# A graph layer on one core: softmax of the last pass made chunk by chunk, one deeper gather ring, and three stages joined

## The reference

```python
xn = layernorm(x)
x = x + relational_gat(xn, src, dst, edge_type)     # 8 heads, softmax over the edges of a node, floored at 0
      + linear_attention(xn)
x = x + shared_mlp(layernorm(x)) + routed_experts(layernorm(x))   # 1024 hidden, 2 of 8 experts
xn = layernorm(x)
h = relu(gcn_conv(xn, src, dst) )                   # self loops, degree norm
x = x + relu(gat_conv(h, src, dst)) + (y := xn + channel_attention(xn)) + mlp(layernorm(y))   # 1 head; 768 hidden
x = x + capacity_ffn(x)                             # top half of the tokens by a router
```

## Time and profile before

| | |
|---|---|
| median of 3 runs | 3726.47 us (3723.8 to 3730.51) |
| the profiled execution | 3732.52 us, span 3730.7 us |
| granted clock, mean | 0.813 of full |
| PE busy | 2577.2 us (69%) |
| DVE busy | 1415.3 us (38%) |
| ACT busy | 1062.6 us (28%) |
| POOL busy | 1368.2 us (37%) |
| instructions | 44933 |

### The profile page before, as it was taken

The page is one execution under the profiler, slowest core; times in us unless marked ns, Lnnn a source line. Parts: engine busy times, 40 slices in busy tenths (PEclk is TensorE's granted clock), DMA queues, the critical chain, the costliest instruction groups (busy, mean ns, idle before and its releaser), DMA issues. The chain is left out here.

```text
span 3730.7 us, 44933 instructions
## 1 busy us (share of the span) xinstructions
PE 2577.2 (69%) x12282; PEld 1921.9 (52%) x12282; DVE 1415.3 (38%) x3375; ACT 1062.6 (28%) x2733; POOL 1368.2 (37%) x1383
## 2 busy tenths in 40 slices
PE   2599626666655778999974577675635667676697
PEld 2465314444434657888863344453434555555575
DVE  4655224544556200000014111222547344444767
ACT  1022213333343111322322243334301333333321
POOL 1022356665640310000013666666230666565110
PEclk7599857777886889999986788787755888888899
DMA  4045433332320102565643333333264222222101
GB/s 161 19 150 184 145 82 93 90 90 81 91 64 25 51 20 84 187 196 179 193 135 103 112 91 91 89 90 92 72 188 142 85 82 84 78 84 78 60 1 35
DMA packets 241044, 370.74 MB, mean 99 GB/s; under 512 B 65140, under 2 KB 171073, under 8 KB 240836
## 3 DMA queue, kind: packets, MB, share of 16 engines
q0 software_dynamic: 63632, 179.42, 16.5%
q1 hardware_dynamic: 147694, 157.81, 13.4%
q10 hardware_dynamic: 29510, 31.06, 2.4%
HBM read 306.56 MB, written 61.61 MB: 99 GB/s over the span
## 5 line engine op out<-in xcount | busy, mean ns | idle before, releaser
L1089 POOL DMA_INDIRECT ag_rows<-rows,e_bsrc x392 | 387.7, 989 | 399.5 <-SPq L1100 257.0
L1307 POOL DMA_INDIRECT at_rows<-values,e_brow x392 | 396.9, 1013 | 282.8 <-SPq L1318 142.1
L2458 POOL DMA_INDIRECT cm_rows<-rows,e_bsrc x392 | 371.0, 946 | 227.7 <-issue 104.9
L1383 PE MATMUL at_part<-at_msg,x 128*128 128x265 f32 x880 | 308.0, 500 | 184.9 <-DVE at_msg L1538 114.7
L1114 PE MATMUL banks<-ag_msg,ag_one 128*128 128x258 f32 x880 | 262.6, 439 | 194.4 <-DVE ag_msg L1146 139.6
L1383 PEld LDWEIGHTS at_part<-at_msg,x 128*128 128x128 f32 x880 | 200.0, 245 | 271.0 <-issue 123.9
L1114 PEld LDWEIGHTS banks<-ag_msg,ag_one 128*128 128x128 f32 x880 | 185.9, 219 | 253.3 <-DVE ag_msg L1146 123.6
L2538 PE MATMUL cm_part<-cm_rows,cm_one 128*128 x880 | 260.3, 444 | 58.3 <-issue 35.1
L1979 POOL DMA_INDIRECT je_y<-expert_out,slots x50 | 48.4, 968 | 648.0 <-POOLq L75 613.9
L2660 DVE TENSOR_TENSOR h<-h,cm_part 128x256 f32 x220 | 92.3, 420 | 461.7 <-PE cm_part L2538 210.0
L2538 PEld LDWEIGHTS cm_part<-cm_rows,cm_one 128*128 128x128 f32 x880 | 184.9, 222 | 122.3 <-issue 96.3
(11 more groups left out here) (602 smaller groups left out, 4264.3 us busy)
## 6 DMA issues: line engine op xcount, KB each, us to landing
x_w<-in_L_ffn_W1p SPq DMA_DIRECT2D x32, 1024.0 KB
x_w<-in_L_ffn_W2p SPq DMA_DIRECT2D x32, 1024.0 KB
values<-p_hv ACTq DMA_DIRECT2D x25, 1088.0 KB
p_brow<-local_row SPq DMA_DIRECT2D x44, 320.0 KB, 3.6
xn_acc<-local_row SPq DMA_DIRECT2D x44, 320.0 KB
xn_acc<-low_row SPq DMA_DIRECT2D x49, 256.0 KB
expert_in<-z_z POOLq DMA_DIRECT2D x8, 1024.0 KB
x_xr<-expert_in SPq DMA_DIRECT2D x32, 256.0 KB, 2.7
```

The lines of the kernel that those rows point to most:

```text
L1089: pool.indirect_dma_start(rows[:, b % slots, k, :], None, table, bass.IndirectOffsetOnAxis(index[:, k, b:b + 1], 0)).then_inc(gathered[b % ...
L1307: pool.indirect_dma_start(rows[:, b % RING, k, :], None, table, bass.IndirectOffsetOnAxis(e.block_row[:, k, b:b + 1], 0)).then_inc(gathere ...
L1383: last = pe.matmul(part[:, n % deep, 0:wide], one[:, n // U % 2, k, n % U, :], msg[:, n % 4, k, :], start=(k == 0), stop=(k == K2 - 1))
L2458: pool.indirect_dma_start(rows[:, b % SLOTS, k, :], None, table, bass.IndirectOffsetOnAxis(e.block_src[:, k, b:b + 1], 0)).then_inc(gather ...
```

## The change

1. `find_groups` no longer makes the tables for `segment_softmax` (DVE L604 to L615, L642 to L660) nor stores `low_row`.
2. `finish_attention0`, `layer_norm` "ln1_", the weight loads and `route_and_share` become one stage. SP starts the loads at its start. DVE `prepare(g)` divides, joins and normalises one group of five tiles at a time (POOL takes the power); PE transposes the first five tiles and starts the MLP; the other 20 tiles are turned between the MLP's steps, the logits come at step 27, the exponential at 29, and the placing matmuls after tile 10 where they came after tile 2.
3. The convolution's ring has 20 blocks, asked back nine late (14 and five before).
4. The `ff1_` weights are loaded by SP in the last pass, behind its 44 loads of rows.
5. `score2`, `segment_softmax` and `aggregate` go; `attend_last` takes their place. Only the 44 destination units are matched; the source score travels as the 257th column of `rows2` (a row is 1028 B, before 1024 B) and ACT fetches it for each pair; the softmax is made online in 14 chunks as in `attend`, with masks brought by DMA from ACT's queue; the ring is 28 blocks freed 22 late. The exponentials now stand between the Gelus of the ride, and an ACT_TABLE_LOAD comes with each switch: 54 by the written order. The ride's down product has one PSUM bank where it had two, and `gcn_to_gat` splits four operations less on `own`.

The diff, cut to its core:

```diff
-SLOTS = 14
-SLOTS2 = 20
-LAG = 5
+SLOTS = 20
+LAG = 9
@@ find_groups @@
-            sp.wait_ge(low_made, 1)
-            for h in range(2):
-                sp.dma_start(low_row[h * BH:(h + 1) * BH], low[:, h, :]).then_inc(rows_out, 16)
...
-            link(dve.tensor_scalar(edge[:], edge[:], NEG, None, ALU.mult))
-            link(dve.tensor_copy(e.step[:], edge[:]))
...
-            link(dve.tensor_scalar(e.over_this[:], this[:], -1.0, -NEG, ALU.add, ALU.mult))
             dve.wait_ge(runs_kept, 1)
@@ MlpRide.multiply @@
                 pe.wait_ge(self.shaped, (lo // 2 + 1) * self.fb)
-                if t >= 2:
-                    pe.wait_ge(self.added, t - 1)
-                else:
-                    pe.wait_ge(*self.gate)
+                if t:
+                    pe.wait_ge(self.added, t)
                 for f in range(self.fb):
-                    last = pe.matmul(self.down_ps[:, t % 2, 0:D], self.hid[:, f, (t - lo) * P:(t - lo + 1) * P], w2[:, f, :],
+                    last = pe.matmul(self.down_ps[:, 0:D], self.hid[:, f, (t - lo) * P:(t - lo + 1) * P], w2[:, f, :],
                                      start=(f == 0), stop=(f == self.fb - 1))
                 last.then_inc(self.down, 1)
+def attend_last(nc, c, e, target, local_row, table, acc, ride, loads):
+    deep = 3
+    wide = D + 2
+    step_of = {lo - LEAD + i: (pc, lo, m, i) for pc, (lo, m) in enumerate(CHUNKS) for i in range(LEAD + 1)}
...
+        @block.sync
+        def _(sp):
+            units = local_row.rearrange("(b g) e -> b (g e)", g=U)
+            for v in range(UNITS):
+                if v >= 3:
+                    sp.wait_ge(matcher, v - 2)
+                sp.dma_start(brow[:, v % 3, :], units[v:v + 1].broadcast_to([P, BT * P])).then_inc(row_in[v % 3], 16)
+            for to, of in loads:
+                sp.dma_start(to, of, allow_slow_non_contiguous=True).then_inc(ride_loaded, 16)
+            for b in range(NB):
+                sp.wait_ge(gathered[b % RING], 16 * K2 * (b // RING + 1))
+                sp.sem_inc(ready, 1)
+                if FREE <= b < NB - RING + FREE:
+                    pairs = sp.value_load(e.upto[0:1, b - FREE:b - FREE + 1], min_val=1, max_val=G)
+                    sp.wait_ge(weighted, pairs)
+                    sp.sem_inc(freed, 1)
+
+        @block.tensor
...
+            for v in range(UNITS):
+                match(v)
+            for n in range(-LEAD, G):
+                if n in step_of:
+                    softmax(*step_of[n])
+                if n < 0:
+                    continue
+                if n == 0:
+                    pe.wait_ge(ride_loaded, 16 * len(loads))
+                ride.multiply(pe, n)
+                if n % U == 0:
+                    pe.wait_ge(hot, n // U + 1)
+                pe.wait_ge(weighted, n + 1)
+                if n >= deep:
+                    pe.wait_ge(summed, n - deep + 1)
+                for k in range(K2):
+                    last = pe.matmul(part[:, n % deep, 0:wide], one[:, n // U % 2, k, n % U, :], msg[:, n % 4, k, :], start=(k == 0), stop=(k == K2 - 1))
+                last.then_inc(multiplied, 1)
+        @block.scalar
...
+            def take_mask(pc):
+                lo, m = CHUNKS[pc]
+                for h, first, past in pieces[pc]:
+                    act.dma_start(mask[first - lo:past - lo, pc % 2, :], e.pair[first - h * HALF:past - h * HALF, h, :]).then_inc(mask_in[pc % 2], 16)
+            def fetch(n):
+                pc, j = n // CH, n % CH
+                if n % U == 0:
+                    blks[:] = several(nc, mybir.EngineType.Activation, e.blk, n, U, NB - 1, waited=True)
+                b = blks[n % U]
+                if j == 0 and pc >= 2:
+                    act.wait_ge(scored, pc - 1)
+                act.wait_ge(ready, b + 1)
+                act.copy(src[:, pc % 2, :, j:j + 1], rows[:, bass.ds(b % RING, 1), :, D:D + 1].squeeze(1)).then_inc(copied, 1)
...
+                if i == 3:
+                    act.wait_ge(shifted, pc + 1)
+                    act.activation(s[0:m], s[0:m], ACT.Exp, scale=-1.0).then_inc(exped, 1)
+                if i == 4:
+                    if pc >= 2:
+                        act.wait_ge(weighted, CHUNKS[pc - 1][0])
+                    act.wait_ge(back_turned, pc + 1)
+                    act.copy(w[:, pc % 2, :, 0:m, :].rearrange("p k n z -> p z k n"),
+                             turn[:, 0:2 * K2 * m].rearrange("p (z k n) -> p z k n", z=2, k=K2)).then_inc(w_kept, 1)
+                    if pc + 2 < len(CHUNKS):
+                        take_mask(pc + 2)
+                if i == 6:
+                    act.wait_ge(faded, pc + 1)
+                    if pc:
+                        act.wait_ge(rescaled, pc)
+                    act.activation(fade[:], small[:, 0:1], ACT.Exp).then_inc(fade_kept, 1)
...
+            act.wait_ge(ride_loaded, 16 * len(loads))
+            for n in range(FREE - LEAD):
+                fetch(n)
+            for n in range(-LEAD, G):
+                if n == -LEAD + 1:
+                    hots(0)
+                if n >= 0 and n % U == 0 and n + U < G:
+                    hots(n // U + 1)
+                if n + FREE < G:
+                    fetch(n + FREE)
+                if n in step_of:
+                    softmax(*step_of[n])
+                if n >= 0:
+                    ride.shape(act, n)
         @block.vector
...
+            def weigh(n, b):
+                pc, j = n // CH, n % CH
+                if n >= 4:
+                    dve.wait_ge(multiplied, n - 3)
+                if j == 0:
+                    dve.wait_ge(w_kept, pc + 1)
+                row = rows[:, bass.ds(b % RING, 1), :, 0:D].squeeze(1)
+                of = w[:, pc % 2, :, j, :]
+                dve.tensor_copy(msg[:, n % 4, :, D:wide], of)
+                dve.tensor_tensor(msg[:, n % 4, :, 0:D], row, of[:, :, 0:1].broadcast_to([P, K2, D]), ALU.mult).then_inc(weighted, 1)
+            def add_up(n, tile):
+                if n:
+                    dve.wait_ge(summed, n)
+                if n % CH == 0:
+                    pc = n // CH
+                    dve.wait_ge(fade_kept, pc + 1)
+                    dve.tensor_scalar(acc[:, tile, :], acc[:, tile, :], fade[:, 0:1], None, ALU.mult).then_inc(rescaled, 1)
+                    dve.wait_ge(rescaled, pc + 1)
+                dve.wait_ge(multiplied, n + 1)
+                dve.tensor_tensor(acc[:, tile, :], acc[:, tile, :], part[:, n % deep, 0:wide], ALU.add).then_inc(summed, 1)
...
+            prepare(0)
+            for v in range(UNITS):
+                if v + 1 < UNITS:
+                    prepare(v + 1)
+                keep(v)
+            dve.wait_ge(cleared, 1)
+            dve.wait_ge(ride_loaded, 16 * len(loads))
+            blks, tiles = [], []
+            for n in range(-LEAD, G + 2):
+                if n in step_of:
+                    softmax(*step_of[n])
+                if 0 <= n < G:
+                    if n % U == 0:
+                        blks = several(nc, mybir.EngineType.DVE, e.blk, n, U, NB - 1)
+                    weigh(n, blks[n % U])
+                    ride.add(dve, n)
+                if n >= 2:
+                    if (n - 2) % U == 0:
+                        tiles = several(nc, mybir.EngineType.DVE, e.tile, n - 2, U, NT)
+                    add_up(n - 2, tiles[(n - 2) % U])
-def route_and_share(nc, c, xnt, x, xn, wr, weights, best, slots, expert, rows):
+def route_and_share(nc, c, acc, degree, xnt, x, xn, router, weights, loads, best, slots, expert, rows):
+    turn_at = {2 + t: t for t in range(U, NT)}
+    points = w2.shape[1] + U
+    route_at = NT + 2
+    PLACED = 2 * U
+    assert route_at + 2 < 2 * points + w2.shape[1] + 1
...
+            def beside(s):
+                if s in turn_at:
+                    turn_tile(turn_at[s])
+                if s == route_at:
+                    pe.wait_ge(router_loaded, 16)
+                    pe.wait_ge(kept, NT)
+                    for t in range(NT):
+                        for k in range(DC):
+                            last = pe.matmul(logit_ps[:, t * NX:(t + 1) * NX], xnt[:, k, t * P:(t + 1) * P], wr[:, k, :],
+                                             start=(k == 0), stop=(k == DC - 1))
+                    last.then_inc(logits_made, 1)
+            for t in range(U):
+                turn_tile(t)
+            pe.wait_ge(loaded, 16 * len(loads))
             for j in range(NT // U):
+                pe.wait_ge(kept, (j + 1) * U)
...
-                    if t == 2:
+                    if t == PLACED:
                         pe.wait_ge(counted, 1)
...
+            pool.memset(minus_half[:], -0.5).then_inc(preset, 1)
+            pool.wait_ge(preset, 1)
+            for g in range(NT // U):
+                of = slice(g * U, (g + 1) * U)
+                pool.wait_ge(varied, g + 1)
+                pool.tensor_tensor(mo.r0[:, of], mo.var[:, of], minus_half[:], ALU.pow).then_inc(rooted, 1)
...
```

(38 more changed lines are left out.)

729 lines of the change are left out of this document (263 added, 466 removed).

## The result

The changed kernel takes 3776.67 us (median of 4, 3767.54 to 3781.28), the kernel before 3725.14 (3717.78 to 3730.51): a ratio of 1.0139, 95% interval 1.012 to 1.0157. It is 1.4% slower, clear of the noise, where 3725 was forecast. The profiled execution has a span of 3779.5 us against 3730.7, 48.8 more.

| stretch | before | after | difference | forecast |
|---|---|---|---|---|
| up to the first layer's first gather | 439.9 | 435.1 | -4.8 | -4.8 |
| first layer's pass | 711.3 | 717.9 | +6.6 | 0 |
| to the convolution's first gather (norm, routing, MLP, experts, join) | 894.1 | 880.1 | -14.0 | -27 |
| convolution | 599.1 | 606.9 | +7.8 | 0 |
| `gcn_to_gat` | 50.5 | 50.8 | +0.3 | -1.1 |

A forecast was written before the change was run, and what follows sets the result against it. No engine was taken as full in any gather pass; PE idles, largely awaiting DVE's messages. Terms -4.8, -1.1, -27, 0, -28.7 and +60.7 summed to -0.9, giving 3725 us at the median, range 3655 to 3785.

The forecast's parts named there:

- rival (1): Last pass's loop: softmax chain adds on top of PE, idle 235 stays, loop 697, time 3760 or more; chance 0.22.
- The prediction's own sign of being wrong: Last pass: forecast wrong if the loop's idle PE time is far from 200 us or matching units don't take 1.4.
- Groups: Table building in find_groups on DVE: removing the segment_softmax tables saves 4.8 us, ends 0 and -7.1.
- gcn_to_gat: Stage before the last pass: the split of `own` goes, five small operations on 25 columns, -1.1 us.
- Joined stage: First layer's finish, norm, routing, MLP: MLP starts at 1171, PE work 204, idle 46, end 1421; -27 us.
- Convolution: Deeper ring: at best 21.7 us of block waits won, against 15 us of added back-to-back gathers; taken as 0.
- Start of the last pass: First gather to first message: gather burst, 44 matching units, weights, fetches and first softmax sum to 159 us; -28.7.
- the burst: Start of the last pass: 28 blocks, 56 gathers at 1.26 us each, 70 us.
- The loop: Last pass's loop with online softmax and ride: PE busy 462, length 662 against 601.3; +60.7 us.
- the middle between 627 and 697: Last pass's loop: 626.8 if added PE work fills idle time, 697 if idle stays whole; 662 taken.
- Rival (2): Last pass's loop: ride runs in PE's idle time, loop 627, time 3690; chance 0.20.
- Rival (3): Longer gather bursts starve all engines: last pass's start saves nothing, convolution +15, time 3769; chance 0.07.

The follow-up runs named there:

- fixed_tile: Changed kernel with the matching units' tile numbers as constants 0 to 4 instead of five register loads per unit on PE: ratio 1.0136 to the kernel before.
- the control: The changed kernel itself, unedited, run again beside three other runs on the first kind of chip: ratio 1.0153 to the kernel before, loop 678.4 us.
- one_table: Changed kernel with the ride's Gelu replaced by Exp, so no table is switched in the last pass: ratio 1.0167 to the kernel before, loop 670.4 us.
- after_lead10: Changed kernel with the last pass's softmax started ten pairs ahead instead of six, blocks asked back 26 late: ratio 1.0161 to the kernel before, other kind of chip.
- after_mended: Changed kernel with ring 14, spaced scatters, spaced first gathers and ACT's softmax step first: ratio 1.0167 to the kernel before, other kind of chip.
- after_paced: Changed kernel with the last pass's first 28 blocks' gathers spread over the 44 matching units: ratio 1.023 to the kernel before, other kind of chip.

## Why the prediction was wrong

The forecast was 3725 within 3655 to 3785, with chances of 0.43 for faster, 0.16 for no change and 0.41 for slower. The time lies in the range by luck: the range reached up to 3785 for rival (1), with PE's idle time kept whole and table loads on the path, and neither happened. What failed are the sizes of four terms of the sum, the joined stage, the convolution, the start of the last pass and the loop, all mis-sized towards faster. The prediction's own sign of being wrong showed: the matching units were to take 1.4 us and took 1.86. PE's idle time in the loop, 210 us, was as forecast. Step by step:

- **Groups** -4.8: measured -4.8. The mechanism is right; that it fits to a tenth is luck, as the first gather comes at 439.8 to 440.4 in the kernels without this change on the first kind and at 434.6 to 437.7 in those with it. **gcn_to_gat** -1.1: +0.3, too small to tell.
- **Joined stage**, -27, measured -14.0 and alone -15.3. From the first layer's pass's end to the MLP's first matmul it took 18.2 us, 2 less than in the sum; that both have the MLP start at 1171 is a coincidence, since the sum counted on from the old end at 1151. What failed is PE's work, put at 204 and 212.4 in the run. The logits took 17.7 where 12.6 stood in the sum, and the ups, taken as unchanged, rose from 440 to 467 ns on average: behind the holes a group of eight takes 3.86 and 4.30 us, elsewhere 2.42. PE's idle time was 51.7 for 46. I wrongly took the stall behind the scatter as given: spaced, it went.
- **Convolution** 0, measured +7.8 (8 to 15 over the runs). The mechanism for a loss was written beside it (12 more gathers back to back, 15 us) and then set to nothing. Of the 21.7 us of waits for blocks 15 were indeed won, and 15 more of unexplained idle time took their place.
- **Start of the last pass**, -28.7, measured -14.4. The mis-sized terms are the unit, 1.39 us by the rate of transfer and 1.86 as measured (53 forecast, 66.8 taken), and the burst, after which DVE stood until 2770 (70 forecast, 79.6 taken); what follows was 11 us shorter than I had. I divided bytes by the rate of a window, which gives the limit that fixed_tile ran into, and didn't write out the longer chain DVE, PE, DVE of one unit with PE's register loads.
- **The loop**, +60.7, measured +67.0 and more (678 in the control). The way was right, PE's busy time as well (460 for 462). What failed is the middle between 627 and 697, which put 35 us on the first layer's loop of 626.8. Without the ride the new loop is 618.6, 8 us under that; the ride puts 51 to 60 on it.
- **Rival (1)** gave table loads up to 69 us: one_table says 0. PE's idle time didn't stay at 235 either, though the loop came close to the 671 from which this rival was to count. **Rival (2)** is out: the ride's work did not vanish in the idle time. **Rival (3)**, the longer bursts, had 0.07 and was half right: it fits what the convolution lost, though no run spaces those gathers, and spacing gave 47.6 us behind the scatter and 41.8 at the start of the last pass. I read the frozen rows, and the earlier trace rows, as a price to be carried over and not as the thing to be removed.

What stays open: whether and how ACT's order takes 20 us out of the loop while DVE's wait stays, what makes some chips freeze, and whether the mended new pass would reach the old on the first kind of chip.

## What to carry to other kernels

When POOL issues indirect transfers back to back, look at what the other engines do in those microseconds; if they stand, let each transfer wait for a step of the work beside it. Two added waits did that here and took the ratio from 0.9958 to 0.9746, some 79 us, more than any part of the change. And before joining two jobs in one loop whose engines all look half idle, take each of them out once: this loop charged the softmax whole and the ride about half. Cost a short step both by its bytes and by its chain of hand-offs, and take the longer: 1.39 us and 1.86 us here.

## What the runs showed of the hardware

The same kernel takes 3718 to 3737 us on one kind of chip and 3232 on another. On the first, other engines stand while POOL issues indirect DMAs back to back: PE for 43 us while 50 scatters are issued, and the start of the last pass takes 186 us where it takes 144 otherwise. On the other, PE is busy 64.2 of 66 us during the same scatter, and the convolution runs at the gathers' 1.25 us each. Each issue takes POOL about the same on both (0.96 to 0.98 us for a scatter, 0.30 between). Where POOL issues nothing, both kinds run alike (PE busy 468.1 and 467.6 of 480 us).

A change that is tuned on one kind says little of the other. On the first kind the two spacings are worth 2% (0.9958 to 0.9746). On the other the joined stage with spaced scatters gives 0.9955 and with the spaced start as well 0.9948; the scatter's spacing shortens its stage by 3 us there, the start's by 1. The new pass loses on both: 1.4 to 1.5% on the first (the changed kernel), and on the other 1.6 to 2.3% in its forms after_lead10, after_mended and after_paced; the changed kernel itself wasn't run there.

Clock: the loop of the last pass had a granted clock of 0.84 with the ride and 0.71 without it, and taking out the ride's 174 us of matmuls lowered PE's busy time by 94 us only. Table switches: 53 switches between exp and gelu took ACT 1.32 us each and the loop nothing. Register loads: with five on PE ahead of a unit's ten matmuls, which take their tile from these registers, a unit took 1.86 us; with fixed tiles it took 1.37.
